# Rounded three-part products replaced by unrounded ones in column halves, in a fused attention and expert kernel

## The chip, the cores and the metric

The kernel runs on one core of one Trainium2 chip. The time is that of one execution on the device, in microseconds (us), as the median of several runs. The trace is one further execution, recorded by the hardware profiler.

## What is computed

Four residual stages work on `x` of 4 batches x 512 tokens x 128 features, with a context of 4 x 32 rows. Cut to what matters:

```
x = x + attn0(ctx, layernorm(x))      # 16 heads of 64; queries, keys and values as below
x = x + ffn0(layernorm(x))            # 8 experts, one for each token, 128 -> 2*512 -> 128, silu gate
x = x + attn1(layernorm(x), ctx)      # 16 heads of 8
x = x + ffn1(layernorm(x))            # 8 experts, the best two, 128 -> 2*256 -> 128

# attn0
q = lat @ Wq;  k, v = split(concat([x, lat]) @ Wkv)
dots = einsum('bhid,bhjd->bhij', q, k) * 64**-0.5
out = einsum('bhij,bhjd->bhid', softmax(dots), v) @ Wout
```

In the first attention the queries come from the 512 tokens of a batch (the call passes the normalised x as `latents`), and the keys and values from the 32 context rows and the 512 tokens. All is float32 at the reference's precision. A router picks experts by comparing logits, so the products ahead of it have to be close to float32.

## The kernel before

All tensors but the lists of tokens stay on the chip. Each of the five engines runs its own program; semaphores join them. The list `order_a`, made at lines 369 to 416 and walked by every engine, sets the order of the first attention. A *pair* is two heads of 64, which fill the 128 partitions of a tile; there are 32 pairs (4 batches x 8), and one round of `ITERATION` (line 320) works on pair i and prepares pair i+1. The 512 keys of a batch are four *key tiles* of 128. Per round, on TensorE, in this order:

- `V` (line 1552): values of one key tile of the next batch, in 16 of the rounds. Features of 128 tokens times 1024 columns of Wv, as two products of 128x128x512.
- `qk` (line 1577): queries and keys of pair i+1, one product of 128x128x512 each.
- `p0` to `p3` (line 1652): exponentials of pair i-1 times values, for each key tile and head one matmul of 128 rows by 64 columns, unrounded, into two halves of bank 6.
- `t0` to `t4` (line 1588): scores of pair i+1 from rounded operands, with queries on the partitions, only to find the maximum of each row.
- `s0` to `s3` (line 1615): the scores of pair i with keys on the partitions, less the row's maximum, for the exponential.
- `rows`, `mt`, `OUT`, the context's parts and the router of the batch before fill the rest.

Precision is kept by splitting. A tensor is rounded to float32r (high part, `QH`, `KH`, `XTH`, `WH`), and VectorE subtracts it from the whole for the low part (`QL`, `KL`, `XTL`, `WL`). A product is then three rounded matmuls, made by `three`:

```
def three(dst, aH, aL, bH, bL):
    pe.matmul(dst, aH, bH, start=True, stop=False)
    pe.matmul(dst, aH, bL, start=False, stop=False)
    return pe.matmul(dst, aL, bH, start=False, stop=True)
```

It is used for queries and keys, values, and the context's keys. The scores have four steps for each key tile (line 1629): KH with QH, KL with QH, KH with QL, and MINUS with TOPROW, which subtracts the maximum. Each step is two matmuls of 64 rows by 128 columns, one for each head, on the two halves of the array's rows.

ScalarE makes QH, KH and the whole query QF from PSUM (lines 843 to 847), VectorE makes KL and QL (lines 1244, 1247). The weights arrive in `PT`, and `round_weights` and `rest_of_weights` split them at the start. Unrounded products on all of the array stand in the output projection (line 1729), the routers' logits (1744, 1844), the experts' first layer (1463, eight products of 128x128x128 for each of 23 tiles of tokens), the second attention (1784 to 1832), and the experts' second layers (1498) and the last first layer (1468), whose weights are at an address that a register gives.

PSUM has eight banks. Each step in `TAKES_BANKS` takes the next two of banks 0 to 5, in turn (line 409); it waits until what the bank last held has been read, which `release` notes.

In the tables below, a tile on TensorE's array is given as rows*columns; `f32` stands for rounded operands also. An unrounded matmul of the program appears in the trace as two records, a rounded one as one record.

Of the kernel before, what the change touches and what calls it, by code (L numbers as in the profile page):

```python
# [5 lines left out]
F32 = mybir.dt.float32  # L6
F32R = mybir.dt.float32r
# [6 lines left out]
P = 128  # L14
# [27 lines left out]
def build(nc, x, ctx, lnm_g, lnm_b, lnl_g, lnl_b, Wq, Wkv, Wout, rw, rb, w1, w2, cq, ckv, cc, Wr, Wg, Wu, Wd, out):  # L42
# [31 lines left out]
    with ExitStack() as stack:  # L74
# [22 lines left out]
        CTH = sb("CTH", P, dt=F32R)  # L97
        CTL = sb("CTL", P, dt=F32R)
# [21 lines left out]
        WA = PT[:, 0:2, :, :].rearrange("p a k n -> p (a k n)")[:, 0:3 * INNER]  # L120

# [35 lines left out]
        with ExitStack() as first:  # L157
            def sb1(name, *shape):
                return first.enter_context(nc.sbuf_tensor(name, [P, *shape], F32R))


            WH = sb1("WH", 3, INNER)
            WL = sb1("WL", 3, INNER)

            XTH = sb1("XTH", 2, S)
            XTL = sb1("XTL", 2, S)

            QH = sb1("QH", 2, S)
            QL = sb1("QL", 2, S)
            KH = sb1("KH", 2, S)  # L170
            KL = sb1("KL", 2, S)
# [5 lines left out]
        XG = sb("XG", RING, ROW)  # L177
        PASSED = sb("PASSED", TILES_D, E)
# [4 lines left out]

        WS = sb("WS", 4, BANK)
        YS = sb("YS", 8, P)
# [74 lines left out]
        CTD = Steps(sem("ctx_dve"), ["ct", "low", "raw"])  # L260
        s_cth = sem("ctx_high")
        XTD = Steps(sem("features_dve"), ["feat", "low"])
        s_xth = sem("features_high")
        s_wh, s_wl = sem("weights_high"), sem("weights_low")
# [5 lines left out]
        s_qk, s_qkh, s_qkl = sem("queries_keys"), sem("qk_high"), sem("qk_low")  # L270
# [63 lines left out]
        for b in range(B + 1):  # L334
# [6 lines left out]
            if b + 1 < B:  # L341
# [4 lines left out]
                put(i + 3, "D", "a_split", b + 1)  # L346
# [134 lines left out]
        def sync_program(sp):  # L481
            sp.dma_start(CTX, ctx.rearrange("b m d -> (b m) d")).then_inc(ld_ctx, 16)
            sp.dma_start(X[:, 0:TPB, :], x_v[:, 0]).then_inc(ld_x[0], 16)
            sp.dma_start(WA[:, INNER:2 * INNER], Wkv[:, 0:INNER]).then_inc(ld_wk, 16)
            for i, v in enumerate((lnl_g, lnl_b, lnm_g, lnm_b)):
                sp.dma_start(GROWS[i:i + 1, :], v.rearrange("(a d) -> a d", a=1)).then_inc(ld_g, 16)
            sp.dma_start(WA[:, 0:INNER], Wq).then_inc(ld_wq, 16)
            sp.dma_start(WA[:, 2 * INNER:3 * INNER], Wkv[:, INNER:2 * INNER]).then_inc(ld_wv, 16)
# [29 lines left out]
            sp.wait_ge(s_qk, ALL)  # L518
# [9 lines left out]
            gates_of(0, E - 1)  # L528

            sp.wait_ge(s_sc, len(scored))  # L530
            gates_of(E - 1, E)
# [210 lines left out]
        def scalar_program(act):  # L742
# [14 lines left out]
            def round_weights(w, ld):  # L757
                act.wait_ge(ld, 16)
                act.activation(WH[:, w, :], WA[:, w * INNER:(w + 1) * INNER], ACT.Copy).then_inc(s_wh, 1)

# [4 lines left out]
            def keep_weights(j):  # L765
                if j in (0, EARLY[0]):
                    act.wait_ge(*(TABLES if j else EARLY_TABLES).at(0, "w_of"))
                if j == 0:
                    act.wait_ge(ld_w1, 48)
# [1130 lines left out]
```

## Time and profile before

| what | value |
|---|---|
| median of 3 runs | 791.95 us (790.49 to 792.25) |
| span of the profiled execution | 788.3 us |
| TensorE (PE) busy | 706.3 us, 90% |
| VectorE (DVE) busy | 475.7 us, 60% |
| ScalarE (ACT) busy | 378.0 us, 48% |
| GpSimd (POOL) busy | 377.4 us, 48% |
| instructions | 13872 |

The span is cut into stages by what runs: set-up to about 30 us, the first attention to about 515, the first experts to about 603, the second attention to about 695, the second experts to the end. Busy times are of records; matmuls are pipelined, so a record's length is more than the time by which it moves the next one. An engine's idle time matters where the chain that ended last passes through it.

### The profile page before, as it was taken

How to read it: one execution, taken by the hardware profiler on the slowest of the kernel's cores; microseconds unless marked ns; L12 is line 12 of the kernel's file. 1: busy time of each engine (PE TensorE's matmuls, PEld its weight loads, DVE VectorE, ACT ScalarE, POOL GpSimd, SP SyncE). 2: the span in 40 equal slices, each digit the busy share in tenths (PEclk: the TensorE clock that was granted, in tenths of full speed). 3: DMA queues.
4: the chain of work that ended last, by engine and by line, in shares of the span. 5: the costliest groups of instructions: out<-in, count | busy, mean ns of one | idle time of the engine just before them, and what ended most of it. 6: DMA issues, size and time to landing. Idle time of an engine off the chain costs nothing.

```text
span 788.3 us, 13872 instructions
## 1 busy us (share of the span) xinstructions
PE 706.3 (90%) x4810; PEld 430.8 (55%) x4810; DVE 475.7 (60%) x966; ACT 378.0 (48%) x580; POOL 377.4 (48%) x361
## 2 busy tenths in 40 slices
PE   4899999999999999999999999997995687568991
PEld 3654555545556555556545545566995343336661
DVE  4745484585585875667477478465443386845553
ACT  4475554564654554655445444344552643223440
POOL 7264453473464475444464553634333304674552
PEclk9999999999999999999999999998998697569996
DMA  9999999990000000000030004301212500122325
GB/s 253 197 201 197 204 190 10 4 4 1 1 1 2 1 14 1 1 1 1 1 121 2 1 1 108 114 24 32 72 32 80 155 1 28 35 75 69 88 66 177
DMA packets 109867, 50.62 MB, mean 64 GB/s; under 512 B 44804, under 2 KB 103048, under 8 KB 109800
## 3 DMA queue, kind: packets, MB, share of 16 engines
q1 hardware_dynamic: 106280, 42.46, 36.0%
q0 software_dynamic: 3520, 7.27, 2.7%
q8 instruction: 42, 0.69, 0.4%
q14 instruction: 25, 0.20, 0.1%
HBM read 20.07 MB, written 29.64 MB: 63 GB/s over the span
## 4 chain that ended last, share of the span: by engine, by line
PE 74%; DVE 11%; issue 5%; ACT 3%; POOL 3%; DMA 2%; another core or an unknown queue 1%; SPq 1%; DVEq 0%; POOLq 0%; ACTq 0%
PE PSUM L1631 14%; PE PSUM L1663 13%; PE PSUM L1598 5%; PE PSUM L1463 5%; PE PSUM L1498 4%; PE PSUM L1468 4%; PE PSUM L1729 4%; PE PSUM L1423 3%; PE PSUM L1425 2%; PE PSUM L1424 2%; PE PSUM L1612 2%; PE PSUM L1605 2%; PE PSUM L1649 2%; PE PSUM L1693 2%; DVE REC L1377 1%
## 5 line engine op out<-in xcount | busy, mean ns | idle before, releaser
L866 ACT ACTIVATE PT<-PSUM 128x1024 f32<-128x1024 f32 x128 | 128.6, 1024 | 134.1 <-PE PSUM L1631 133.7
L690 POOL TENSOR_TENSOR PSUMS<-PT 128x1024 f32<-128x1024 f32 x32 | 76.0, 2376 | 210.4 <-ACT PT L866 171.4
L690 POOL TENSOR_TENSOR PSUMS<-PSUMS,PT 128x1024 f32<-128x1024 f32 x62 | 149.6, 2413 | 16.8 <-ACT PT L866 9.9
L1254 DVE TENSOR_REDUCE TOPS<-PSUM 128x2 f32<-128x1024 f32 x128 | 152.1, 1220 | 6.9 <-PE PSUM L1598 6.5
L1663 PE MATMUL PSUM<-PT,BIG 128*64 128x512 f32 x512 | 130.6, 611 | 0.0
L1209 DVE TENSOR_TENSOR SIL<-SIL,PSUM 128x256 f32<-128x256 f32 (+1 forms) x62 | 32.2, 519 | 65.7 <-ACT SIL L783 46.8
L1244 DVE TENSOR_TENSOR KL<-PSUM,KH 128x512 fp32r<-128x512 f32 x32 | 22.1, 691 | 68.2 <-ACT KH L844 67.7
L1598 PE MATMUL PSUM<-KH,QH 64*128 64x512 f32 x256 | 57.9, 449 | 4.0 <-DVE QL L1247 3.7
L1663 PEld LDWEIGHTS PSUM<-PT,BIG 128*64 128x64 f32 x512 | 28.4, 135 | 53.4 <-issue 52.0
L1598 PEld LDWEIGHTS PSUM<-KH,QH 64*128 64x128 f32 x256 | 24.2, 183 | 59.2 <-DVE TOPS L1254 24.9
L783 ACT ACTIVATE SIL<-PSUM 128x256 f32<-128x256 f32 (+1 forms) x62 | 28.6, 462 | 56.7 <-PE PSUM L1463 31.4
L1631 PE MATMUL PSUM<-QH,KH 64*128 64x512 f32 x256 | 54.8, 423 | 1.0 <-DVE QL L1247 0.7
L662 POOL DMA_INDIRECT results_d<-YS,XG x39 | 37.4, 958 | 29.4 <-DVE YS L1216 27.3
L1631 PE MATMUL PSUM<-TOPROW,MINUS 64*128 64x512 f32 x256 | 51.1, 393 | 0.0
L1631 PE MATMUL PSUM<-QH,KL 64*128 64x512 f32 x256 | 50.9, 391 | 0.0
L1631 PE MATMUL PSUM<-QL,KH 64*128 64x512 f32 x256 | 50.8, 390 | 0.0
L1463 PE MATMUL PSUM<-XGT,WS 128*128 128x128 f32 x368 | 46.8, 282 | 0.4 <-issue 0.4
L1463 PEld LDWEIGHTS PSUM<-XGT,WS 128*128 128x128 f32 x368 | 44.5, 198 | 1.0 <-issue 0.8
L1468 PE MATMUL PSUM<-BIG,XGT 128*128 x78 | 42.7, 631 | 1.9 <-DVE XGT L1201 1.9
L662 POOL DMA_INDIRECT results_b<-YS,XG x23 | 22.0, 957 | 36.9 <-DVE YS L1216 35.7
L1293 DVE TENSOR_TENSOR OT<-OT,PSUM 128x1024 f32<-128x1024 f32 x16 | 18.9, 1217 | 34.0 <-PE PSUM L1680 34.0
L655 POOL DMA_INDIRECT lists_d<-BIG,SLOT x28 | 27.2, 971 | 12.0 <-issue 7.9
(256 smaller groups left out, 1365.5 us busy)
## 6 DMA issues: line engine op xcount, KB each, us to landing
lists_d<-EMPTY SPq DMA_DIRECT2D x3, 2730.0 KB, 35.3
lists_b<-EMPTY SPq DMA_DIRECT2D x3, 2470.0 KB, 33.4
lists_d<-EMPTY SPq DMA_DIRECT2D x1, 2665.0 KB, 34.9
XG<-lists_d SPq DMA_DIRECT2D x39, 65.0 KB
lists_b<-EMPTY SPq DMA_DIRECT2D x1, 2405.0 KB, 17.2
BIG<-in_L_ffn_w SPq DMA_DIRECT2D x1, 2048.0 KB
W2ALL<-in_L_ffn_w SPq DMA_DIRECT2D x4, 512.0 KB, 6.2
PT<-results_d SPq DMA_DIRECT2D x8, 256.0 KB, 4.4
```

The costliest lines, as they stand in the source:

```text
L662: pool.indirect_dma_start(RES[which], bass.IndirectOffsetOnAxis(ap=XG[:, g % RING, D:D + 1].bitcast(U32), axis=0), YS[:, g % 8, :], None). ...
L690: pool.tensor_tensor(PSUMS[:, i % 2], PTT[:, i % 2, 0] if kt == 1 else PSUMS[:, i % 2], PTT[:, i % 2, kt], ALU.add).then_inc(s_ps, 1)
L866: act.activation(PTT[:, i % 2, kt], PSUM[:, place:place + 2, :], ACT.Exp, scale=DH ** -0.5).then_inc(s_exp, 1)
L1209: dve.tensor_tensor(sl, sl, up, ALU.mult).then_inc(s_hid, 1)
L1254: dve.tensor_reduce(TOPS[:, c, 0, :], PSUM[:, place:place + 2, :], AX.X, ALU.max).then_inc(s_max, 1)
L1463: last = pe.matmul(PSUM[:, bank + n, c:c + P], WS[:, 2 * (g % 2) + n, c:c + P], XGT[:, g % 3, :], start=True, stop=True)
L1468: last = pe.matmul(PSUM[:, bank, :], XGT[:, g % 3, :], WGUALL[:, bass.ds(column[1][j], BANK)], start=True, stop=True)
L1498: last = pe.matmul(PSUM[:, bank, 0:D], hidden[:, f * P:(f + 1) * P], weights[:, f * D:][:, bass.ds(column[which][j], D)], start=f == 0, st ...
L1598: last = pe.matmul(PSUM[:, place + h, :], QH[r, i % 2, c * P:(c + 1) * P], KH[r, i % 2, :], start=True, stop=True)
L1631: last = pe.matmul(PSUM[:, place + h, :], lhs, rhs, start=step == 0, stop=step == 3)
L1663: last = pe.matmul(PSUM[DH * h:DH * h + DH, 6, :], V[:, b % 2, kt, cols], PTT[:, i % 2, kt, h, :], start=kt == 0, stop=kt == KT - 1)
L1729: last = pe.matmul(PSUM[:, place, t * P:(t + 1) * P], OT[:, (GROUP * a + c) % OTS, t * P:(t + 1) * P], WOUT[:, (GROUP * a + c) % PAIRS, :] ...
```

## The change

1. `three` goes. A new helper makes an unrounded product as two matmuls of 64 columns, into partitions 0 to 63 and 64 to 127 of the result. It is used for queries and keys, values, the context's keys, the first layer of the first experts (1463), the output projection, the routers' logits, and the matmuls of the second attention.
2. The scores have two steps: KF with QF, unrounded, as two halves of 64 columns for each head (four tiles of 64x64), and MINUS with TOPROW, rounded, as before.
3. ScalarE makes QH and QF, VectorE KH and KF (a whole copy of the keys). The two halves of `qk` count on semaphores of their own (`s_qp`, `s_kp`), and their banks are released apart. The maxima's matmuls wait for QH and for KH, the scores for QF and KF.
4. The weights are no longer split. They are loaded into a tensor `WA` of their own, and the context's values use them in one step. The features are written once, as `XF`. `a_split` goes.
5. The tensors' places in memory change, and the loads of w1's gates are cut in four (experts 0 to 2, 4 to 6, 3, 7), the last two after the last scores, since those read QF and TOPROW to their end.

```diff
+            def halves(dst, stationary, moving, start=True, stop=True):
+                for n in range(0, P, 64):
+                    last = pe.matmul(dst[n:n + 64], stationary[:, n:n + 64], moving, start=start, stop=stop)
+                return last
...
                     for n in range(2):
-                        c = slice(n * BANK, (n + 1) * BANK)
-                        last = three(PSUM[:, place + n, :], XTH[:, k, cols], XTL[:, k, cols], WH[:, 2, c], WL[:, 2, c])
+                        last = halves(PSUM[:, place + n, :], XF[:, k, cols], WA[:, 2, n * BANK:(n + 1) * BANK])
...
-                    for w in range(2):
-                        last = three(PSUM[:, place + w, :], WH[:, w, c], WL[:, w, c], XTH[:, k, :], XTL[:, k, :])
-                    last.then_inc(s_qk, 1)
-                    release(mine, (s_qkl, 2 * a + 2))
+                    for w, made in enumerate((s_qp, s_kp)):
+                        halves(PSUM[:, place + w, :], WA[:, w, c], XF[:, k, :]).then_inc(made, 1)
+                    release(mine[0:1], (s_qf, a + 1))
+                    release(mine[1:2], (s_kf, a + 1))
...
                     if c == 0:
-                        pe.wait_ge(s_qkh, 3 * i + 2)
+                        pe.wait_ge(s_qh, i + 1)
+                        pe.wait_ge(s_kh, i + 1)
...
-                    for step in range(4):
-                        if (kt, step) == (0, 3):
+                    for step in range(2):
+                        if (kt, step) == (0, 1):
                             pe.wait_ge(s_toprow, i + 1)
                         for h in range(2):
                             r = slice(DH * h, DH * h + DH)
-                            c = slice(kt * P, (kt + 1) * P)
-                            lhs = (KH[r, k, c], KL[r, k, c], KH[r, k, c], MINUS[r, :])[step]
-                            rhs = (QH[r, k, :], QH[r, k, :], QL[r, k, :], TOPROW[r, i % GROUP, :])[step]
-                            last = pe.matmul(PSUM[:, place + h, :], lhs, rhs, start=step == 0, stop=step == 3)
+                            if step == 0:
+                                halves(PSUM[:, place + h, :], KF[r, k, kt * P:(kt + 1) * P], QF[r, i % GROUP, :], stop=False)
+                            else:
+                                last = pe.matmul(PSUM[:, place + h, :], MINUS[r, :], TOPROW[r, i % GROUP, :], start=False, stop=True)
...
                     for f in range(2 * FF // P):
                         n, c = divmod(f * P, BANK)
-                        last = pe.matmul(PSUM[:, bank + n, c:c + P], WS[:, 2 * (g % 2) + n, c:c + P], XGT[:, g % 3, :],
-                                         start=True, stop=True)
+                        last = halves(PSUM[:, bank + n, c:c + P], WS[:, 2 * (g % 2) + n, c:c + P], XGT[:, g % 3, :])
...
                 elif name == "qk":
-                    dve.wait_ge(s_qkh, 3 * a + 2)
-                    dve.tensor_tensor(KL[:, a % 2, :], PSUM[:, place + 1, :], KH[:, a % 2, :].bitcast(F32),
-                                      ALU.subtract).then_inc(s_qkl, 1)
-                    dve.wait_ge(s_qkh, 3 * a + 3)
-                    dve.tensor_tensor(QL[:, a % 2, :], PSUM[:, place, :], QH[:, a % 2, :].bitcast(F32), ALU.subtract).then_inc(s_qkl, 1)
+                    dve.wait_ge(s_kp, a + 1)
+                    if a >= 2:
+                        dve.wait_ge(s_sc, scores_of(a - 2))
+                    dve.tensor_copy(KH[:, a % 2, :], PSUM[:, place + 1, :]).then_inc(s_kh, 1)
+                    dve.tensor_copy(KF[:, a % 2, :], PSUM[:, place + 1, :]).then_inc(s_kf, 1)
```

On TensorE, in the first rounds of the pair loop, this stands before, from the keys' product to the third key tile of `p` (names stand as moving, stationary; `PT,BIG` is the product with the values, whose tensor V lies in BIG; `KH,QH` a matmul of the maxima; the rest are the three parts of the keys' product and the four score steps):

```order
L1423 MATMUL PSUM<-XTH,WH 128x512
L1424 MATMUL PSUM<-XTL,WH 128x512
L1425 MATMUL PSUM<-XTH,WL 128x512
L1663 MATMUL PSUM<-PT,BIG 64x512 x4
L1598 MATMUL PSUM<-KH,QH 128x512 x2
L1631 MATMUL PSUM<-QH,KH 128x512 x2
L1631 MATMUL PSUM<-QH,KL 128x512 x2
L1631 MATMUL PSUM<-QL,KH 128x512 x2
L1631 MATMUL PSUM<-TOPROW,MINUS 128x512 x2
L1598 MATMUL PSUM<-KH,QH 128x512 x2
L1663 MATMUL PSUM<-PT,BIG 64x512 x2
```

and this now, at the same place (line 1367 is the new helper's matmul; 64x512 is the result of one half):

```order
L1552 MATMUL PSUM<-IDENT,TOPT 128x128 x4
L1367 MATMUL PSUM<-XF,WA 64x512 x4
L1604 MATMUL PSUM<-PT,BIG 64x512 x4
L1538 MATMUL PSUM<-KH,QH 128x512 x2
L1367 MATMUL PSUM<-QF,KF 64x512 x4
L1572 MATMUL PSUM<-TOPROW,MINUS 128x512 x2
L1538 MATMUL PSUM<-KH,QH 128x512 x2
L1604 MATMUL PSUM<-PT,BIG 64x512 x2
```

No step changed its place; six matmuls of 128 columns became four of 64, and the three rounded score steps four quarters, with a matmul of 64 rows by 128 columns ahead of them and behind.

On VectorE, between two pairs, this stands before (from the joined maxima of one pair to those of the context for the next):

```order
L1265 TENSOR_REDUCE TOPT<-TOPS 128x4x2
L1244 TENSOR_TENSOR KL<-PSUM,KH 128x512
L1247 TENSOR_TENSOR QL<-PSUM,QH 128x512
L1254 TENSOR_REDUCE TOPS<-PSUM 128x2 x4
L1256 TENSOR_REDUCE TOPS<-PSUM 128x2x4
```

and now:

```order
L1212 TENSOR_REDUCE TOPT<-TOPS 128x4x2
L1193 CAST KH<-PSUM 128x512
L1194 COPY KF<-PSUM 128x512
L1201 TENSOR_REDUCE TOPS<-PSUM 128x2 x4
L1203 TENSOR_REDUCE TOPS<-PSUM 128x2x4
```

Two subtractions that came after ScalarE's roundings became two copies straight from PSUM, of which the first is an operand of the next matmuls of the maxima.

## Rows read from the trace of the kernel before

**Rows 1.** The page: busy us (share) xinstructions, and the clock in 40 slices.

```profile
PE 706.3 (90%) x4810; PEld 430.8 (55%) x4810; DVE 475.7 (60%) x966; ACT 378.0 (48%) x580; POOL 377.4 (48%) x361
...
PEclk9999999999999999999999999998998697569996
```

**Rows 2.** The page: the chain that ended last, by engine and by line.

```profile
PE 74%; DVE 11%; issue 5%; ACT 3%; POOL 3%; DMA 2%; another core or an unknown queue 1%; SPq 1%; DVEq 0%; POOLq 0%; ACTq 0%
PE PSUM L1631 14%; PE PSUM L1663 13%; PE PSUM L1598 5%; PE PSUM L1463 5%; PE PSUM L1498 4%; PE PSUM L1468 4%; PE PSUM L1729 4%; PE PSUM L1423 3%; PE PSUM L1425 2%; PE PSUM L1424 2%; PE PSUM L1612 2%; PE PSUM L1605 2%; PE PSUM L1649 2%; PE PSUM L1693 2%; DVE REC L1377 1%
```

**Rows 3.** Stretches: start:end length, busy of each engine, clock, DMA share, GB/s.

```profile
300.00:400.00 100.00, 100.00 (x688) 56.65 (x688) 64.06 (x96) 51.57 (x70) 44.77 (x22) 1.00 0.00 1
...
560.00:610.00 50.00, 42.19 (x376) 41.81 (x375) 18.96 (x50) 22.84 (x29) 16.27 (x17) 0.97 0.18 53
```

**Rows 4.** Waits of PE from 30 to 515 us, the largest.

```profile
PE PSUM L1598 <- DVE QL L1247: 3.7, 5, 0.7
```

**Rows 5.** Timeline of PE, one pair: start, length, line, out<-in, tile, shape, records.

```profile
326.90 0.39 PE L1425 MATMUL PSUM<-WH,XTL 128*128 128x512 f32 x1
327.13 0.40 PE L1423 MATMUL PSUM<-WH,XTH 128*128 128x512 f32 x1
...
329.29 1.94 PE L1663 MATMUL PSUM<-PT,BIG 128*64 128x512 f32 x8
331.15 0.51 PE L1598 MATMUL PSUM<-KH,QH 64*128 64x512 f32 x2
331.50 0.40 PE L1631 MATMUL PSUM<-QH,KH 64*128 64x512 f32 x2
...
332.43 0.40 PE L1598 MATMUL PSUM<-KH,QH 64*128 64x512 f32 x2
332.76 1.08 PE L1663 MATMUL PSUM<-PT,BIG 128*64 128x512 f32 x4
333.77 0.50 PE L1598 MATMUL PSUM<-KH,QH 64*128 64x512 f32 x2
334.11 0.39 PE L1631 MATMUL PSUM<-QH,KH 64*128 64x512 f32 x2
```

**Rows 6.** Timeline of PE in the last stage: an unrounded product on all columns.

```profile
736.32 1.02 PE L1468 MATMUL PSUM<-BIG,XGT 128*128 x2
737.18 0.27 PE L1447 MATMUL PSUM<-IDENT,XG 128*128 128x128 f32 x1
```

**Rows 7.** Timeline of PE: one rounded product between two other shapes.

```profile
225.93 0.50 PE L1598 MATMUL PSUM<-KH,QH 64*128 64x512 f32 x2
226.36 0.65 PE L1419 MATMUL PSUM<-IDENT,NRM 128*128 128x128 f32 x4
```

**Rows 8.** Timeline of PE: eight tiles of 64x32 at once, two steps.

```profile
312.92 1.09 PE L1649 MATMUL PSUM<-QF,KCF 64*32 64x512 f32 x16
313.80 1.06 PE L1649 MATMUL PSUM<-TOPROW,MINUS 64*32 64x512 f32 x16
314.80 0.50 PE L1423 MATMUL PSUM<-XTH,WH 128*128 128x512 f32 x1
```

**Rows 9.** The chain in order of time: the context's values.

```profile
36.12 3.66 PE PSUM L1571 x64
```

**Rows 10.** Timeline of PE: the first product of the queries, with its wait.

```profile
15.34 0.80 PE L1423 MATMUL PSUM<-XTH,WH 128*128 128x512 f32 x1 [2.29 <-DVE XTL L966]
```

**Rows 11.** Timeline of PE in the first experts: one tile's first layer.

```profile
564.83 1.95 PE L1463 MATMUL PSUM<-XGT,WS 128*128 128x128 f32 x16
566.62 0.27 PE L1447 MATMUL PSUM<-IDENT,XG 128*128 128x128 f32 x1
```

**Rows 12.** Costliest groups: busy, mean ns, then idle before and what ended it.

```profile
L1244 DVE TENSOR_TENSOR KL<-PSUM,KH 128x512 fp32r<-128x512 f32 x32 | 22.1, 691 | 68.2 <-ACT KH L844 67.7
```

More of the change, by code:

```diff
@@ L259, in build @@
         s_tr = sem("lane_turned")
[L260 to L264, printed above, removed]
+        CTD = Steps(sem("ctx_dve"), ["ct", "raw"])
+        s_xf = sem("features")
         s_const_r = sem("rounded_consts")
@@ L1743, in tensor_program @@
                     for t in range(TPB):
-                        last = pe.matmul(PSUM[:, place, t * E:(t + 1) * E], XT[:, t * P:(t + 1) * P], RW[:, 0, :],
-                                         start=True, stop=True)
+                        last = halves(PSUM[:, place, t * E:(t + 1) * E], XT[:, t * P:(t + 1) * P], RW[:, 0, :])
                     last.then_inc(RP0.sem, 1)
@@ L1783, in tensor_program @@
                     claim(6)
-                    pe.matmul(PSUM[:, 6, :], WC[:, 0, :], FEAT[a], start=True, stop=True).then_inc(CPP[a].sem, 1)
+                    halves(PSUM[:, 6, :], WC[:, 0, :], FEAT[a]).then_inc(CPP[a].sem, 1)
                     free[6] = CPA[a].at(0, "q")
@@ L1793, in tensor_program @@
                             r = slice(32 * c, 32 * c + 32)
-                            last = pe.matmul(PSUM[:, c, t * P:(t + 1) * P], QT[a][r, t * P:(t + 1) * P], KBD[r, a, :, :],
-                                             start=True, stop=True)
+                            last = halves(PSUM[:, c, t * P:(t + 1) * P], QT[a][r, t * P:(t + 1) * P], KBD[r, a, :, :])
                     last.then_inc(CPP[a].sem, 1)
@@ L1812, in tensor_program @@
                             r = slice(32 * c, 32 * c + 32)
[L1813 to L1814 removed]
+                            last = halves(PSUM[:, c, :], (KBD[r, a, :, :].rearrange("p h k -> p (h k)"), MINUSC[r, :])[step],
+                                          (QT[a][r, :], TOPROWC[r, :])[step], start=step == 0, stop=step == 1)
                     last.then_inc(CPP[a].sem, 1)
@@ L1831, in tensor_program @@
                     for t in range(TPB):
-                        last = pe.matmul(PSUM[:, 7, t * P:(t + 1) * P], OC[:, a % 2, t * P:(t + 1) * P], WC[:, 1, :],
-                                         start=True, stop=True)
+                        last = halves(PSUM[:, 7, t * P:(t + 1) * P], OC[:, a % 2, t * P:(t + 1) * P], WC[:, 1, :])
                     last.then_inc(CPP[a].sem, 1)
@@ L1843, in tensor_program @@
                     for t in range(TPB):
-                        last = pe.matmul(PSUM[:, 7, t * E:(t + 1) * E], FEAT[a][:, t * P:(t + 1) * P], RW[:, 1, :],
-                                         start=True, stop=True)
+                        last = halves(PSUM[:, 7, t * E:(t + 1) * E], FEAT[a][:, t * P:(t + 1) * P], RW[:, 1, :])
                     last.then_inc(RP1[a].sem, 1)
```

147 lines of the change are left out of this document (47 added, 100 removed).

## The prediction, made before the changed kernel ran

> **What bounds the kernel now.** Read first the busy time by engine and the clock row [rows 1]: TensorE is busy for 706.3 us of 788.3, and the clock row shows full speed everywhere but in the last quarter. Then the chain that ended last [rows 2]: 74% of it is TensorE's, and the lines with the largest shares are the score matmuls (L1631, 14%), the product with the values (L1663, 13%), the row maxima (L1598, 5%) and the experts' first layer (L1463, 5%). The table by stretches says where this holds [rows 3]: from 300 to 400 us TensorE is busy for all of 100 us, at a granted clock of 1.00 (the 2.4 GHz level), while VectorE is busy for 64, ScalarE for 52 and GpSimd for 45; in the experts' stage (560 to 610) it is 42 of 50. The waits of TensorE between 30 and 515 us have 3.7 us in their largest entry [rows 4]. So in the first attention, which is more than 60% of the span, there is nearly no slack on TensorE, and each microsecond of its work added or removed there moves the end by as much. The others have a third to a half of their time free. The change is therefore counted in TensorE's start-to-start times.
>
> **Four prices, from one pair of heads** [rows 5]. The timeline merges instructions, so the price of a group is the start of the next group less its own start.
> - A rounded product (float32r) of 512 columns: L1425 starts at 326.90, the next at 327.13: 0.23 us. A product of three such is 0.69. The two 64-row matmuls of the two heads run at once: four score steps take 331.50 to 332.43, 0.93 us, 0.23 each.
> - An unrounded product (float32) on all 128x128 of the array: L1468 appears as two records, 736.32 to 737.18, 0.86 us [rows 6].
> - The same as two of 64 columns side by side: L1663 is in that form already. Two key tiles, that is two products of 128x128x512 in eight records, take 329.29 to 331.15, 1.86 us; one takes 332.76 to 333.77, 1.01. The difference is 0.85 to 0.86 a product. So splitting the columns leaves an unrounded product at 0.86 us, and it stays 0.17 dearer than three rounded ones.
> - Changing the shape of the tile on the array. Around one key tile of L1663 (128x64), between products of 64x128: L1598 takes 0.33 to the start of L1663 where 0.23 is usual (+0.10), L1663 takes 1.01 for 0.86 (+0.15), and the L1598 behind it takes 0.35 and elsewhere 0.33 to 0.34 (+0.11). A visit to another shape and back costs 0.36 us. The price is no smaller when visits follow one another: one rounded product alone between two other shapes takes 225.93 to 226.36, 0.43 us, that is 0.23 + 0.10 + 0.10 [rows 7].
>
> **Scores, 32 pairs x 4 key tiles = 128 key tiles.** Before: 0.93 us each. Now the product of KF and QF is four 64x64 quarters. Eight tiles of 64x32, unrounded, did run at once: the two steps of L1649 take 312.92 to 313.80 (0.88) and 313.80 to 314.80 (1.00, with a change of shape) [rows 8]. I take that four 64x64 tiles do so too: 0.86. Behind it comes one rounded product, MINUS with TOPROW, in 64x128: 0.23. The shape goes to 64x64 and back: 0.36. Sum 1.45, which is +0.52 each, x128 = **+66.6 us**. The 64x64 tile itself is in no row. Its bounds: no cost of the change from 64x64 to 64x128, since both have 64 rows, +0.16 a tile, +20.5 us in all; and quarters that run two and two, 0.86 more a tile, +177 us. I take 0.36 for the change, because every change in the rows is paid (in [rows 8] 64x32 to 128x128, and is the nearest).
>
> **Queries and keys, 32 pairs.** Two products, 2 x (0.86 - 0.69) = 0.34 a pair, **+10.9 us**. No change of shape is added: the one ahead of L1663 moves ahead of the queries, since these are 128x64 now as L1663 is. **Values, 16 tiles,** also two products each: **+5.4 us**.
>
> **Context values** (L1571) were unrounded products with the high and with the low part of the weights, 3.66 us [rows 9]; one set goes: **-1.8 us**. The eight context keys are 128 columns wide: +0.17/4 each, 0.3 us, double at the slow clock of the start. **The start:** L1423 waited 2.29 us for the low part of the features [rows 10], and this split is gone with its two steps; the first two products are then longer. I take **-1 us** for all of the start, bounds -3 and +1.
>
> **Experts' first layer** (L1463, 23 tiles of 8 products with 128 columns moving) [rows 11]. 16 records take 564.83 to 566.62, 1.79 us, 0.11 each. In halves each has half the columns and two run side by side; I take 0.11 for two. But the shape goes to 128x64 and back once a tile, at most 0.36 us; 23 of these are 8 us at most, and 7.8 us of 50 are idle in this stretch. **+6 us**, bounds 2 and 8. Output product (L1729), logits, second attention: the same work in another shape, mostly next to a change of shape that is there already or off the path, **+1 us**, bounds -1 and 5.
>
> **VectorE and ScalarE.** VectorE exchanges two subtractions of 0.69 us for two copies from PSUM of the same size; ScalarE loses one copy a pair. The one new wait: the row maxima (top) now need KH from VectorE, before from ScalarE. Queued ahead on VectorE may be normalising and reciprocals. But VectorE stood idle 68.2 us ahead of 32 L1244, 2.1 us each, until ScalarE had made KH [rows 12], so it is free when the keys are done, and the matmuls of L1663 (1.86 us) cover the 0.7. I cost it at 0; with no cover in a quarter of the pairs it is 5 us. The loads of w1's gates go out in one more part, and the parts for experts 3 and 7 wait for the last scores; before, expert 7's waited so too, and the last values, sums and reciprocals stand between that and its first use: 0.
>
> **Sum:** 66.6 + 10.9 + 5.4 - 1.8 - 1 + 6 + 1 = 87.1. TensorE's small idle time in the attention takes up about 1. The profiled span is 788.3 and the median of the runs 791.95, so 3.65 lie around it and are not touched. 788.3 + 86 + 3.65 = **878 us**.
>
> The Trainium skill (TensorEngine Tiling, Theoretical Speedup) says that a dimension of 64 or less brings up to 2x by tiling. By it one would halve the price of each half product. Here the full product has 128 columns, and the trace has 0.86 for it in either form; the rule is met only if it's read for matrices that are small to begin with. It is the first rival below.
>
> **Rivals.**
> 1. *Faster: side by side, both records of both halves go through in 0.43.* It decides if the 64-column pair of the changed kernel takes half of what L1663 takes. Then queries, keys and values fall to 0.43 a product: (0.69 - 0.43) x 96 = -25; the scores are 0.43 + 0.23 + 0.36 = 1.02, +0.09 x 128 = +12; L1463 and L1729 lose half of 41 and 28 us, -34; with +4 for the rest, -43: 749 us. Against it stand 512 records of L1663 at the full price. 3%.
> 2. *A change between 64x64 and 64x128 is free or half as dear*, as both split the rows alike: 833 us if free, 856 at half. For it: no row has this pair. Against: every other pair of shapes pays. 10%, most of it on the dearer half.
> 3. *Narrow products lose in halves.* With 128 columns moving, the loading of weights may set the pace, and two loads of 64 columns may not overlap. Half again on the 0.11 of L1463 (368 records) and L1729 (256) is +34, with more at 50: 912 to 928. 5%.
> 4. *The quarters of one head wait for each other*: up to +110 us, 988. 3%.
> 5. *VectorE's KH comes late* in many pairs: +5 to +10, 883 to 888, within the range. 5%.
>
> **How the numbers follow.** The forecast has 74%, with a range of 862 to 893 of its own from the bounds of the experts, the start and 0.30 to 0.40 for a visit. The range 850 to 897 holds it, rival 5 and the dearer half of rival 2: about 85%. Faster by over 0.2% (some 1.6 us, about what a measurement of this kernel can tell from none): 3%, rival 1. Within 0.2%: 1%. Slower: 96%.
>
> **What would show it.** In the changed kernel's timeline: the four quarters and the rounded product take about 1.45 us from start to start of the next key tile, 0.43 between the two waves of the quarters; two 64-column products of 512 take 1.72; TensorE is still at 99 to 100% in the attention and its 32 pairs take some 80 us longer; L1463 takes 1.8 us a tile with 0.1 to 0.15 on either side; the experts' second stage at the end is unchanged. The prediction is wrong if a quarter wave takes other than 0.43, if the next product starts with no gap behind the quarters, or if TensorE waits for KH or KF.

## The result, and the profile after

| | kernel before | changed kernel |
|---|---|---|
| median of the runs beside one another | 792.1 us (790.49 to 793.02, 4 runs) | **875.96 us** (867.71 to 876.66, 4 runs) |
| span of the profiled execution | 788.3 us | 874.8 us |

The changed kernel takes 1.1024 times as long (95% interval 1.097 to 1.1079). The forecast was 878.0.

The page of the changed kernel: busy time by engine, the clock in 40 slices, the chain that ended last, and two of the costliest groups (busy us, mean ns, then the idle time ahead and what ended it).

```profile
span 874.8 us, 16401 instructions
...
PE 780.1 (89%) x6058; PEld 357.4 (41%) x6058; DVE 471.5 (54%) x958; ACT 357.4 (41%) x540; POOL 373.7 (43%) x361
...
PEclk9999999999999999999999999999799698659997
...
PE 79%; DVE 7%; another core or an unknown queue 4%; issue 4%; ACT 2%; DMA 2%; POOL 1%; SPq 0%; POOLq 0%; DVEq 0%; ACTq 0%
PE PSUM L1367 35%; PE PSUM L1604 12%; PE PSUM L1572 6%; PE PSUM L1538 5%; PE PSUM L1440 4%; PE PSUM L1410 4%; PE PSUM L1552 2%; PE PSUM L1545 2%; PE PSUM L1590 2%; PE PSUM L1634 2%; PE PSUM L1390 1%; PE PSUM L1361 1%; PE PSUM L1425 1%; PE PSUM L1659 1%
...
L1367 PE MATMUL PSUM<-QF,KF 64*64 64x512 f32 x1024 | 139.4, 615 | 0.0
...
L1193 DVE CAST KH<-PSUM 128x512 fp32r<-128x512 f32 x32 | 22.1, 690 | 69.7 <-PE PSUM L1367 69.4
```

TensorE is busy 74 us longer, ScalarE 21 less, VectorE and GpSimd 4 less each. The span is 86.5 longer. Line 1367, the matmul of the new helper, now holds 35% of the chain; in [rows 2] the largest line held 14%. "Another core or an unknown queue" has gone from 1% to 4%; this is taken up under the second attention below.

Where the time went is read by cutting both traces at the same events on TensorE: the first matmul of the maxima, the last product with the values, the first and last matmul of the first experts, the first and last of the second experts.

| stretch, us | before | after | difference | forecast |
|---|---|---|---|---|
| start | 20.2 | 17.0 | -3.2 | -1 (-3 to +1) |
| first attention | 495.7 | 567.3 | +71.6 | +80.1 |
| from there to the first experts | 10.6 | 10.4 | -0.2 | 0 |
| first experts | 76.3 | 86.2 | +9.9 | +6 (2 to 8) |
| second attention | 95.7 | 103.3 | +7.6 | +1 (-1 to +5), with logits and output |
| second experts | 75.1 | 75.8 | +0.7 | 0 |
| end | 14.7 | 14.9 | +0.2 | 0 |

The forecast's 80.1 for the attention is 66.6 + 10.9 + 5.4 - 1.8, less the 1 us of idle time. The total is right, and three of its terms are not: the attention came out 8.5 us cheaper, and the two stages behind it about 10 dearer.

The tables by stretches, first of the changed kernel, then of the one before, over the whole of the first attention and of the two stages behind it (start:end length, busy of PE, PEld, DVE, ACT, POOL, granted clock, DMA share, GB/s):

```profile
17.00:584.30 567.30, 559.58 (x3950) 201.93 (x3950) 320.29 (x463) 242.51 (x322) 247.63 (x133) 1.00 0.42 50
```

```profile
594.70:680.90 86.20, 78.72 (x969) 70.11 (x965) 33.72 (x107) 39.83 (x51) 28.70 (x38) 0.92 0.12 35
680.90:784.10 103.20, 53.68 (x658) 28.89 (x658) 61.26 (x207) 35.66 (x74) 38.44 (x58) 0.72 0.21 61
```

```profile
20.20:515.90 495.70, 489.79 (x3383) 269.48 (x3386) 319.86 (x466) 258.44 (x356) 248.12 (x133) 1.00 0.46 55
```

```profile
526.50:602.80 76.30, 71.06 (x591) 69.03 (x589) 33.91 (x107) 39.78 (x51) 28.77 (x38) 0.96 0.14 39
602.80:698.50 95.70, 56.52 (x395) 32.64 (x395) 61.76 (x208) 35.89 (x74) 38.57 (x58) 0.72 0.22 66
```

In the attention the clock is 1.00 in both, and TensorE is busy for 98.6% and 98.8%: it is TensorE's own work that grew by 70 us, with the others' busy time the same or less. In the second attention it is the opposite: TensorE is busy 2.8 us *less* than before, at the same mean clock of 0.72, and the stretch is 7.6 us longer. So it is not more work on TensorE that accounts for it.

One pair in the changed kernel, to be read beside [rows 5] (timeline of PE):

```profile
356.61 1.89 PE L1604 MATMUL PSUM<-PT,BIG 128*64 128x512 f32 x8
358.43 0.50 PE L1538 MATMUL PSUM<-KH,QH 64*128 64x512 f32 x2
358.86 1.09 PE L1367 MATMUL PSUM<-QF,KF 64*64 64x512 f32 x8
359.88 0.50 PE L1572 MATMUL PSUM<-TOPROW,MINUS 64*128 64x512 f32 x2
360.21 0.40 PE L1538 MATMUL PSUM<-KH,QH 64*128 64x512 f32 x2
...
365.23 1.09 PE L1367 MATMUL PSUM<-QF,KF 64*64 64x512 f32 x8
366.24 0.50 PE L1572 MATMUL PSUM<-TOPROW,MINUS 64*128 64x512 f32 x2
366.68 1.09 PE L1367 MATMUL PSUM<-QF,KF 64*64 64x512 f32 x8
```

The key tile at 365.23 ends where the next begins, at 366.68: 1.45 us, as forecast. The one at 358.86 takes 1.35 to 360.21, and the matmul of the maxima ahead of it takes 0.43 in place of the 0.33 to 0.35 of [rows 5]: 1.35 + 0.10, once more 1.45. The eight records of the quarters take 1.02 to the start of `MINUS`. Record by record, the second wave of quarters starts 0.48 after the first, in all of the 128 key tiles, and `MINUS` 0.54 after the second. So the forecast's sign, 0.43 between the waves, is not met to the letter: the first wave of L1604 takes 0.48 too where another shape stands ahead of it (0.43 where none does), and the rest of the change is behind the quarters. The sum of 1.45 holds.

The waits of TensorE between 30 and 585 us have one large entry. In [rows 4] it was 3.7 us for QL, which is gone.

```profile
PE PSUM L1538 <- DVE KH L1193: 6.4, 5, 1.4
```

### The profile page after: what moved, and what is told of

It reads as the page before. It is cut to its first block, busy times and chain, and to the rows that moved or that the text cites. A ratio compares the mean times of both kernels' runs of the same rounds, so it can differ in the third digit from the quotient of the medians.

```text
span 874.8 us, 16401 instructions
## 1 busy us (share of the span) xinstructions
PE 780.1 (89%) x6058; PEld 357.4 (41%) x6058; DVE 471.5 (54%) x958; ACT 357.4 (41%) x540; POOL 373.7 (43%) x361
## 4 chain that ended last, share of the span: by engine, by line
PE 79%; DVE 7%; another core or an unknown queue 4%; issue 4%; ACT 2%; DMA 2%; POOL 1%; SPq 0%; POOLq 0%; DVEq 0%; ACTq 0%
PE PSUM L1367 35%; PE PSUM L1604 12%; PE PSUM L1572 6%; PE PSUM L1538 5%; PE PSUM L1440 4%; PE PSUM L1410 4%; PE PSUM L1552 2%; PE PSUM L1545 2%; PE PSUM L1590 2%; PE PSUM L1634 2%; PE PSUM L1390 1%; PE PSUM L1361 1%; PE PSUM L1425 1%; PE PSUM L1659 1%
## 5 line engine op out<-in xcount | busy, mean ns | idle before, releaser
L1201 DVE TENSOR_REDUCE TOPS<-PSUM 128x2 f32<-128x1024 f32 x128 | 156.6, 1225 | 55.4 <-PE PSUM L1538 54.9
L1367 PE MATMUL PSUM<-QF,KF 64*64 64x512 f32 x1024 | 139.4, 615 | 0.0
L1604 PE MATMUL PSUM<-PT,BIG 128*64 128x512 f32 x512 | 129.1, 605 | 0.0
L1572 PEld LDWEIGHTS PSUM<-TOPROW,MINUS 64*128 64x128 f32 x256 | 23.8, 183 | 103.9 <-issue 103.9
L1367 PE MATMUL PSUM<-XF,WA 128*64 128x512 f32 x256 | 63.2, 615 | 1.0 <-DVE XF L923 0.9
L1572 PE MATMUL PSUM<-TOPROW,MINUS 64*128 64x512 f32 x256 | 64.0, 497 | 0.0
L1538 PE MATMUL PSUM<-KH,QH 64*128 64x512 f32 x256 | 57.3, 445 | 6.5 <-DVE KH L1193 6.4
L1193 DVE CAST KH<-PSUM 128x512 fp32r<-128x512 f32 x32 | 22.1, 690 | 69.7 <-PE PSUM L1367 69.4
L1604 PEld LDWEIGHTS PSUM<-PT,BIG 128*64 128x64 f32 x512 | 31.4, 136 | 60.3 <-issue 59.1
L1367 PE MATMUL PSUM<-XGT,WS 128*64 128x128 f32 x736 | 48.6, 288 | 0.4 <-issue 0.4
L1538 PEld LDWEIGHTS PSUM<-KH,QH 64*128 64x128 f32 x256 | 24.1, 184 | 58.2 <-issue 57.1
L1367 PEld LDWEIGHTS PSUM<-XGT,WS 128*64 128x64 f32 x736 | 42.9, 144 | 3.5 <-issue 1.0
L1367 PEld LDWEIGHTS PSUM<-QF,KF 64*64 64x64 f32 x1024 | 26.6, 131 | 27.2 <-issue 26.5
```

Of the source, the lines that this page charges most:

```text
L1201: dve.tensor_reduce(TOPS[:, c, 0, :], PSUM[:, place:place + 2, :], AX.X, ALU.max).then_inc(s_max, 1)
L1367: last = pe.matmul(dst[n:n + 64], stationary[:, n:n + 64], moving, start=start, stop=stop)
L1538: last = pe.matmul(PSUM[:, place + h, :], QH[r, i % 2, c * P:(c + 1) * P], KH[r, i % 2, :], start=True, stop=True)
L1572: last = pe.matmul(PSUM[:, place + h, :], MINUS[r, :], TOPROW[r, i % GROUP, :], start=False, stop=True)
L1604: last = pe.matmul(PSUM[DH * h:DH * h + DH, 6, :], V[:, b % 2, kt, cols], PTT[:, i % 2, kt, h, :], start=kt == 0, stop=kt == KT - 1)
```

## Experiments

The chips on which these ran differ: the kernel before had a median of 792.1 us beside the changed kernel, 795.7 beside the first four kernels here, 781.9 beside the next three and 780.1 beside the last two. So totals are compared as ratios to the kernel before on the same chip, and causes by the length of the first attention, where TensorE sets the pace at a granted clock of 1.00. Matmuls that no edit touches take the same there in every trace (those that sum the exponentials, 15.03 us in all, in each of the eleven).

| kernel | ratio to before (95%) | attention | first experts | second attention |
|---|---|---|---|---|
| before | 1 | 495.7 | 76.3 | 95.7 |
| changed kernel | 1.1024 (1.097 to 1.1079) | 567.3 | 86.2 | 103.3 |
| e1, scores whole | 1.0541 (1.0471 to 1.061) | 527.0 | 86.0 | 103.4 |
| e2, all whole | 1.0388 (1.0321 to 1.0455) | 528.8 | 78.8 | 97.7 |
| e3, whole behind the attention | 1.0866 (1.0795 to 1.0937) | 566.8 | 81.3 | 93.1 |
| e5, KH on ScalarE | 1.0952 (1.0864 to 1.1039) | 560.9 | 86.0 | 104.0 |
| e6, scores rounded | 1.0191 (1.0156 to 1.0226) | 510.8 | 84.3 | 91.3 |
| e7, before with p3 beside p2 | 1.0183 (1.0146 to 1.0221) | 513.9 | 77.8 | 91.4 |
| e8, before with all of p together | 1.026 (1.0226 to 1.0295) | 516.2 | 79.0 | 92.2 |
| e9, all whole and KH on ScalarE | 1.0348 (1.0301 to 1.0395) | 522.8 | 79.2 | 92.9 |
| e10, scores rounded, rest whole | 1.0095 (1.0071 to 1.0119) | 507.2 | 79.2 | 89.8 |

**e1: what do the quarters cost?** The changed kernel, with the scores' product as 64x128 in place of two 64x64.

```diff
-    halves(PSUM[:, place + h, :], KF[r, k, kt * P:(kt + 1) * P], QF[r, i % GROUP, :], stop=False)
+    pe.matmul(PSUM[:, place + h, :], KF[r, k, kt * P:(kt + 1) * P], QF[r, i % GROUP, :], start=True, stop=False)
```

> The changed kernel, but the product of KF and QF on all 128 columns (tiles of 64x128, one for each head) in place of four quarters of 64x64. The tile's shape is then that of the maxima's matmuls ahead and of the rounded product behind. Theory A (an unrounded product costs 0.86 us in either form, and changing shape there and back costs 0.34): 128 key tiles lose 0.34 each, 43 us less, 832 to 834 us. Rival B (the change of shape between tiles of equal rows is cheap, and the loss lies in the four passes alone): no change, 874 to 877. Rival C (quarters are what makes the unrounded product cheap): slower than 880.

The attention fell by 40.3 us, 0.315 for each of 128 key tiles, where theory A had 43. (The total, 837.7, lies over its 832 to 834; on this chip the kernel before is 3.6 us slower too.) Rivals B and C are out. The timeline of PE, one key tile:

```profile
348.23 0.50 PE L1538 MATMUL PSUM<-KH,QH 64*128 64x512 f32 x2
348.56 1.02 PE L1570 MATMUL PSUM<-QF,KF 64*128 64x512 f32 x4
349.02 0.80 PE L1572 MATMUL PSUM<-TOPROW,MINUS 64*128 64x512 f32 x2
349.66 0.40 PE L1538 MATMUL PSUM<-KH,QH 64*128 64x512 f32 x2
```

From 348.56 to 349.66 is 1.10 us, 0.86 + 0.23, and the matmul of the maxima ahead takes 0.33 again. (The split between the second and the third row, at 349.02, is not that of the work: with two records for an unrounded matmul, the start of the next is put too early. Only the sum over both is used.) Four quarters and two heads at full width do the same work in the same time, and what the quarters cost is the visit: 1.45 - 1.10 = 0.35, less where the neighbour had another shape anyway. Rival 2, a free change between 64x64 and 64x128, is out: both split the rows alike, and the change is paid in full.

**e2 and e3: the other halves.** e2 makes every product of the helper whole:

```diff
-                for n in range(0, P, 64):
-                    last = pe.matmul(dst[n:n + 64], stationary[:, n:n + 64], moving, start=start, stop=stop)
-                return last
+                return pe.matmul(dst, stationary, moving, start=start, stop=stop)
```

> The changed kernel with every unrounded product on all of its 128 columns, so that no product is split. Theory A: as with the scores alone (832), less two changes of shape for each of 23 tiles of the first experts (6 to 8 us), less some in the second attention: 815 to 826. The queries, keys and values gain nothing, since L1604 behind them is 128x64 and the change is then paid there. Rival C (splitting is a gain somewhere): no better than the kernel in which only the scores are on all columns.

e3 leaves the attention's products in halves and makes those of the experts, of the routers and of the second attention whole:

```diff
-     last = halves(PSUM[:, bank + n, c:c + P], WS[:, 2 * (g % 2) + n, c:c + P], XGT[:, g % 3, :])
+     last = whole(PSUM[:, bank + n, c:c + P], WS[:, 2 * (g % 2) + n, c:c + P], XGT[:, g % 3, :])
...
```

> The changed kernel with the split taken back only outside of the attention's products: the first experts' first layer, the output projection, the logits, and the second attention. It prices the part of the loss that lies behind the attention. Theory A: the stage of the first experts returns to 76 us from 86, the second attention by up to 7: 860 to 868 us. Rival (the loss behind the attention is the granted clock's, which falls at other moments in each execution, and not the split's): 873 to 877.

Against e1, e2 has the attention 1.8 us *longer*: queries, keys, values and output products whole are no faster than in halves. They share their shape with the product of the values (128x64) when cut, and pay a change more when whole (3.1 us more at queries, keys and values, 2.2 less at the transposes ahead of the queries). Outside the attention whole is cheaper: the first experts take 78.8 against 86.0 us (e2 and e1), and 81.3 in e3, where 76 had been expected. The totals, 825.96 and 863.15, lie in the ranges of theory A, the first at its edge. The timelines of one tile of tokens, changed kernel:

```profile
630.55 1.97 PE L1367 MATMUL PSUM<-XGT,WS 128*64 128x128 f32 x32
632.45 0.33 PE L1390 MATMUL PSUM<-IDENT,XG 128*128 128x128 f32 x1
632.62 1.06 PE L1440 MATMUL PSUM<-W2ALL,SIL 128*128 x8
633.60 1.97 PE L1367 MATMUL PSUM<-XGT,WS 128*64 128x128 f32 x32
```

A tile takes 3.05 us; before, from 564.83 [rows 11] to the next first layer at 567.62, it took 2.79. The 32 records take 1.90 us where 16 took 1.79, so two halves still go at the price of one whole, and the rest is the two changes. 0.26 x 23 tiles is 6.0 us, the forecast's figure. e2 and e5 had the same mean clock there, 0.96, and are 7.2 us apart, but not all of that is the halves: TensorE waited for SIL for 1.9 us in e2 and for 6.0 in e5.

**e5: who makes KH?** ScalarE rounds the keys, as in the kernel before; VectorE only copies KF.

```diff
+                    act.wait_ge(s_kp, a + 1)
+                    act.activation(KH[:, a % 2, :], PSUM[:, place + 1, :], ACT.Copy).then_inc(s_kh, 1)
...
-                    dve.tensor_copy(KH[:, a % 2, :], PSUM[:, place + 1, :]).then_inc(s_kh, 1)
+                    dve.wait_ge(s_kh, a + 1)
```

> The changed kernel with KH rounded by ScalarE again, as before; VectorE makes KF alone, after it. TensorE waited 6.4 us in five places for KH from VectorE. Theory (these waits are on the path): 5 to 7 us less, 869 to 871. Rival (VectorE is late there with the maxima of the next matmul also, as in the kernel before, where 0.9 us was lost in the same five places, so most of it stays): 1 to 3 us less, 873 to 875.

The total, 870.8, is in the theory's range. The attention fell by 6.4 us, the size of the entry `PE PSUM L1538 <- DVE KH L1193: 6.4, 5, 1.4`, and no wait on KH is left. What the five waits have in common is seen in the changed kernel's timeline at one of them:

```profile
317.44 1.94 PE L1367 MATMUL PSUM<-XF,WA 128*64 128x512 f32 x8
317.55 2.35 DVE L1240 TENSOR_TENSOR OT<-OT,PSUM 128x1024 f32<-128x1024 f32 x2 [5.74 <-PE PSUM L1621]
...
319.21 1.89 PE L1604 MATMUL PSUM<-PT,BIG 128*64 128x512 f32 x8
...
319.93 0.69 DVE L1219 TENSOR_TENSOR REC<-REC,PSUM 64x512 f32<-64x512 f32 x1
320.66 0.94 DVE L1221 RECIPROCAL REC<-REC 64x128 f32<-64x128 f32 x1
321.63 0.69 DVE L1193 CAST KH<-PSUM 128x512 fp32r<-128x512 f32 x1
...
322.47 0.50 PE L1538 MATMUL PSUM<-KH,QH 64*128 64x512 f32 x2 [1.38 <-DVE KH L1193]
```

In this round VectorE first adds the context's share to the output (2.35 us) and then joins the row sums (0.69) and takes reciprocals (0.94), and comes to the keys at 321.63, 2.42 us after the next product had begun. The 1.89 us of L1604 no longer cover it. Such a round is not rare: in 13 of the 32 VectorE stood idle for less than 0.1 us ahead of the keys. In eight of these L1604 still covered the copy; in five TensorE waited.

**e6: how much of it is the scores?** The changed kernel with the four rounded score steps of the kernel before, KL and QL on VectorE, and KH on ScalarE.

```diff
-                    for step in range(2):
-                        if (kt, step) == (0, 1):
+                    for step in range(4):
+                        if (kt, step) == (0, 3):
...
+                            c = slice(kt * P, (kt + 1) * P)
+                            lhs = (KH[r, k, c], KL[r, k, c], KH[r, k, c], MINUS[r, :])[step]
+                            rhs = (QH[r, k, :], QH[r, k, :], QL[r, k, :], TOPROW[r, i % GROUP, :])[step]
+                            last = pe.matmul(PSUM[:, place + h, :], lhs, rhs, start=step == 0, stop=step == 3)
```

> The changed kernel with the scores' four rounded steps of the kernel before (KH, KL, QH, QL made as there); queries, keys, values, and all behind the attention stay in unrounded halves. Theory: 128 key tiles lose 0.5 us each, 57 to 64 us, so 812 to 819 us, and the attention's stretch keeps 8 to 16 us over the 495.7 of the kernel before for the queries', keys' and values' fourth pass (48 x 0.34 = 16, less 2 for the context's values and 3 to 5 for waits of before that longer products may cover). Rival (the unrounded queries, keys and values cost nothing net): the stretch is 494 to 498 us.

The attention is 50.1 us shorter than in e5, which differs from it in the scores and in what is made for them, and 15.1 over the kernel before, within the 8 to 16 expected. But 3.1 of the 15.1 are a single pause ahead of the context's scores, for which the profile names nothing:

```profile
PE PSUM L1593 <- issue: 3.1, 1, 3.1
```

The absolute time, 798.15 us, is below the 812 to 819 expected since this chip runs the kernel before at 781.9.

**e7 and e8: fewer visits in the kernel before.** If a visit to the shape 128x64 costs 0.36 us, products with the values that stand together should save it. e7 is the kernel before with this order:

```diff
-            "E A B PC CA0 C CA1 O0 ADD CS V qk p0 p1 t0 s0 t1 p2 t2 D s1 t3 p3 t4 P0 P2 s2 s3 rows mt O1 OUT "
+            "E A B PC CA0 C CA1 O0 ADD CS V qk p0 p1 t0 s0 t1 p2 p3 t2 D s1 t3 t4 P0 P2 s2 s3 rows mt O1 OUT "
```

> The kernel before, with the product of the third and fourth key tile with the values put next to each other in each round (p2 p3, then t2, s1, t3, t4). Nothing is added or left out; one change to the 128x64 shape and back goes out of each of 32 rounds. Theory (each costs 0.34 us of TensorE's time and TensorE is the bound): 11 us less, 780 to 785. Rival (the maxima's reductions, 1.22 us on VectorE each, no longer have p3 between t2 and t3, and TensorE waits for banks instead): 789 to 797.

and e8 with this:

```diff
-            "E A B PC CA0 C CA1 O0 ADD CS V qk p0 p1 t0 s0 t1 p2 t2 D s1 t3 p3 t4 P0 P2 s2 s3 rows mt O1 OUT "
+            "E A B PC CA0 C CA1 O0 ADD CS V qk p0 p1 p2 p3 t0 s0 t1 t2 D s1 t3 s2 t4 P0 P2 s3 rows mt O1 OUT "
```

> The kernel before, with all four key tiles' products with the values in one run ahead of t0, so that 64x128 work follows in one run to the end of the round. Theory: two changes there and back go out of each round, 22 us less if nothing waits: 770 to 775. Rival (without p2 and p3 between them the maxima's matmuls come each 1.16 us, VectorE needs 1.22 for each, and ScalarE must make three exponentials of 1.02 us in a row): part or all of it is lost, 778 to 795.

Both are slower, by 1.8% and 2.6%; the theory was wrong on the sum. Read from start to start, the products with the values did take 4.7 us less in e7 (124.0 to 119.4) and 9.4 less in e8, 0.15 for each visit saved: the part of a visit's 0.36 that stands in the product itself. But the attention is 18.2 and 20.5 us longer. TensorE stands idle in it for 21.5 and 23.9 us in all, where it was 5.9, and its waits in e7 between 30 and 540 us now begin with

```profile
PE PSUM L1605 <- DVE TOPS L1254: 6.2, 25, 0.3
PE PSUM L1631 <- ACT PT L866: 5.8, 11, 0.8
```

and in e8 with

```profile
PE PSUM L1598 <- DVE TOPS L1254: 8.1, 30, 0.6
PE PSUM L1631 <- ACT PT L866: 5.8, 25, 0.3
```

None of these was among the waits of the kernel before beyond 0.3 us. p3 had stood between two matmuls of the maxima, t3 and t4 (not t2 and t3, as the expectation has it), whose results VectorE reduces, and ahead of scores that ScalarE exponentiates, and gave them the time. The visit is the price of that time. The idle time is 15.5 of e7's 18.2 us; what is left stands mostly in the maxima's matmuls beside the waits, 6.2 us longer, less the 4.7 saved.

**e9: do the two add up?** e2's and e5's edits together.

> The changed kernel with both edits tried so far one at a time: every product that the change cut into two of 64 columns is one of 128, and ScalarE makes the rounded keys KH. If the two costs are independent, the attention is 528.8 us (whole products) less 6.4 us (KH on ScalarE), 522 to 523, and the ratio to the kernel before is 1.0388 less 0.008, 1.031 (1.027 to 1.035). The rival: with whole products the queue of VectorE has less time between keys and maxima than before, so that moving KH gains more than 6.4 us, or the waits had already gone with the shorter scores, and the attention stays within 1 us of 528.8.

The attention is 522.8 us, where 528.8 - 6.4 = 522.4 was expected; the ratio is in the range too. The two costs add up to within 0.4 us.

**e10: what is left without scores and halves?** e6's and e2's edits together: the unrounded products of queries, keys and values stand whole in place of three rounded ones.

> The changed kernel with the four rounded score steps of the kernel before (attention 510.8 us, 15.1 over the kernel before), and now every product that is cut into two of 64 columns made whole as well. What is left of the change is that queries, keys, values and the context's keys are unrounded products on all of the array in place of three rounded ones. Theory: an unrounded product costs 0.86 us in either form, so what the halves cost is the changes of tile shape around them alone (0.1 to 0.2 us for each of 32 pairs and 32 value tiles): the attention is 503 to 508 us, the first experts go from 84.3 to 77 to 79 us, and the ratio is 1.004 to 1.012. Rival: the whole product is cheaper than the halves by itself, by 0.43 us each or more; then the attention falls by over 20 us, under 490, and the kernel is faster than the one before. That the kernel comes out faster in any way is not expected.

507.2 us in the attention and 1.0095, both inside the expected ranges; 11.5 us over the attention before. Queries, keys and values are 14.3 of it, the transposes 1.1, the context's values -1.7, and TensorE's idle time is 2.5 us less. The 3.6 us to e6 are no gain of whole products: TensorE is idle for 7.6 us in e6's attention, pause included, and for 3.5 here. e9 less e10, which differ in the scores, is 15.6 us, and e10 is idle 2.2 us more: with unrounded scores the shape costs 40 us (e1), the fourth pass some 18. e10 is the best of the variants, and still slower than the kernel before. No experiment pointed to a version that beats it.

## Why the prediction came out right, and where it did not

**The four prices held.** An unrounded product is 0.86 us whole or in halves, and a score tile is 1.45 with its changes. The waves of the quarters alone stand 0.48 us apart, not 0.43. The profile was read rightly in this: a row of the product of the values, in a quite different place, told the price of the new form. Rival 1 (halves go through in 0.43) would have made the attention shorter, and it's 71.6 us longer; in e2, halves or whole change it by under 2 us.

By the Trainium skill (TensorEngine Tiling, Theoretical Speedup), a dimension of 64 or less gives up to 2x; here, halves of a dimension of 128 give nothing (0.86 us in either form), which does not contradict it. By the same page (Key Properties), a change of the tiling mode drains TensorE. The trace has time lost at every such boundary, 0.10 us, with 64x64 and 64x128 too, where the rows are split alike; that it goes into a drain, no run shows.

**Scores: the term was 7 us too large.** Read from start to start over all 128 key tiles, a score tile took 1.40 us after and 0.99 before, when the waits for QL are left out (1.02 with them), and the matmuls ahead of it grew by 6 us in all: 53.2 + 6 = 59 us, against 66.6. The step that failed is "before: 0.93 us each". That is the price of a tile between two maxima, like the one at 331.50 in [rows 5], and holds for 57 of the 128. The other 71 have something else ahead or behind and took 1.01 to 1.06 (two of them 1.13): a boundary of 0.1 was being paid at them already, which the new one replaces. e5 less e6, 50.1 us, with the 6.2 us that e6 is idle where e5 is not, is 56; the other 3 stand at queries, keys and the context's scores, which are that much slower in e6.

Such a tile of the kernel before, the timeline of PE where two tiles follow one another and then a transpose:

```profile
353.68 0.48 PE L1631 MATMUL PSUM<-QH,KH 64*128 64x512 f32 x2
...
354.69 0.39 PE L1631 MATMUL PSUM<-QH,KH 64*128 64x512 f32 x2
...
355.39 0.40 PE L1631 MATMUL PSUM<-TOPROW,MINUS 64*128 64x512 f32 x2
355.71 0.55 PE L1612 MATMUL PSUM<-IDENT,TOPT 128*128 128x128 f32 x3
```

353.68 to 354.69 is 1.01, and 354.69 to 355.71 is 1.02.

**Queries, keys and values** came to 6.6 + 4.6, and the transposes of the maxima in front of 64-column products to 3.4 more: 14.6 us against 16.3. **Context values:** -1.7 against -1.8.

**KH on VectorE: costed at 0, is 6.4.** The reason given, 68.2 us of idle time ahead of 32 instructions [rows 12], is a sum, and a mean of 2.1 us hides the 13 rounds in which there was none or under 0.1; in five of them TensorE waits. The price of no cover in a quarter of the pairs had been put at 5, and rival 5 at 5 to 10. Part of it was made good: in five places before, the matmul of the maxima waited until VectorE had made QL ([rows 4]; 4.5 us when read from start to start), and these waits are gone. Net it is about +2. The terms of the attention make 59.4 + 14.6 - 1.7 + 1.9 = 74.2, where 71.6 was measured; the products with the values (-1.1), TensorE's other waits (-0.9), the routers' logits (-0.5) and the context's scores (-0.2) account for the rest.

**The start** gained 3.2 us and not 1; the wait of 2.29 [rows 10] is 0.91 now, the transposes ahead of it start 1.7 us earlier (10.19 for 11.93), and from the first product to the first maxima it is 4.8 us in both. **First experts:** +9.9 against +6. 6.0 is the tiles, as forecast. On a chip without what follows, e6 takes 84.3 with halves and e7 and e8 77.8 and 79.0 with the old code, 5.3 to 6.5 less. Another 2.6 is a wait that the kernel before didn't have, seen in the chain of the changed kernel in order of time:

```profile
609.63 9.47 another core or an unknown queue
...
619.13 0.60 ACT SIL L768
...
619.75 0.70 DVE SIL L1155
...
620.58 2.08 PE PSUM L1440 x8
```

The profile doesn't name what ScalarE waited for, but the trace's semaphore events do: the count that TensorE gives for a finished first layer. The last matmul of that layer ends at 616.68, as modelled; the count came at 619.10. TensorE then waited 2.6 us for SIL. The rest, 1.3 us, is not placed. The granted clock was at its lower level for 13.7 us of this stage (mean 0.92) and for 6.8 before (0.96), which may be it. e5, with 6.8, took as long, but waited for SIL for 6.0 us in all where the changed kernel waited 3.0, so it does not rule the clock out.

**Second attention: +7.6 against +1.** TensorE has no more work in it, as the stretch table shows. In the chain of the changed kernel the largest piece of this stage is

```profile
734.23 10.99 another core or an unknown queue
...
745.24 0.60 ACT OT L901
```

Two more of 3.4 and 3.3 us follow. ScalarE waited for TensorE's count of four transposes: the last ends at 738.65, as modelled, and the count came at 745.21. VectorE waited until 739.44 for one whose matmuls end at 735.03. So what comes late in both engines is TensorE's counts, or its matmuls end later than the profile models them; the trace can't tell which. In the chain before, the piece at this place is

```profile
663.77 2.91 another core or an unknown queue
```

On the chips of e6 to e10 no such piece is in the stage's chain at all, and no count of TensorE comes more than 0.8 us late. There it takes 91.3 us with halves (e6), 91.4 and 92.2 with the old code (e7, e8), and 92.9 and 89.8 whole (e9, e10). So the halves as such cost it nothing that shows beside a scatter of 3 us; on those chips the +1 and its reason stand. On the first chips it was 103.3, 103.4 and 104.0 with halves, 95.7, 97.7 and 93.1 without: there halves go with the longer wait, and the stage lies outside the forecast's -1 to +5, which had no term for it. Why the counts are late stays open. In both kernels GpSimd sends indirect DMAs one after the other at that time; the same DMAs stand in e6's trace, where nothing is late. And the traces of the first chips lack some semaphore events: in this stage 491 are there for the kernel before, and 917 in e7, which issues the same instructions. So the names in the chain are weaker there, and whether the recording itself has a part in the wait, no run tells.

**Around the span** 3.65 us were added, the difference of a median and the span of one execution. In the executions of which both are on record it is 1.7 to 2.8 us, and 876.66 for 874.8 is what came.

So, measured less forecast: -7 on the scores, -2 on the queries and values, +2 on KH, -1.5 on small items of the attention, -2 on the start, +4 and +6.5 in the two stages behind, +1 in the stretches between, and -2 around the span. That 878 was met to 2 us owes as much to their signs as to the working: the two stages behind came out dearer, mostly for something that was not in the forecast, by about what the attention came out cheaper, and that is luck.

## What to carry to other kernels

Price a new form from a row in which the same form already runs, and the old one as the mean over all its places, not from the one place that is easiest to read: its boundaries may already be paid. Splitting a full-width unrounded product into columns buys nothing by itself; what counts is whether its shape is that of its neighbours, since here each boundary between shapes costs 0.1 us or more, and a visit 0.35. And a slack that is read as a sum hides the rounds in which there is none: before a copy moves to another engine, look at what is queued ahead of it in its worst round.

## What was not expected of the hardware

- A change between two shapes that differ only in columns (64x64 and 64x128) costs what any other does: 0.35 us for a visit, 1.45 against 1.10.
- Unrounded halves with only 128 columns moving are no dearer than whole: 32 records in 1.90 us against 16 in 1.79 with a boundary in it, and the output products, 25.5 us in all, did not change.
- Taking visits away made the kernel slower (e7, e8). The visit's matmuls were the cover under which VectorE's reductions and ScalarE's exponentials ran: TensorE's idle time in the attention went from 5.9 to 21.5 and 23.9 us.
- On some chips, at the same code, TensorE's counts come 2 to 7 us after its matmuls should have ended (2.4 and 6.6 us in the places shown), and ScalarE and VectorE stand together for up to 11 us; on others none is over 0.8 us late in five traces. The cause is open.
